# Shared-key attention (L1_ffn) as one stage, from gate logits to the layer norm

## The reference, cut to what matters

```python
x = _layernorm(x + _L1_ffn_ref(x, L1_ffn_W_gate, L1_ffn_W_qkv))   # H = 16 heads, hd = 16

gating = softmax(x @ W_gate.T)
idx = argmax(gating);  indicator = one_hot(idx, H)
gating_top1 = indicator * max(gating)
q, k, v = split(x @ W_qkv.T, 3)
k_shared = einsum('bth,bthd->btd', indicator, k)      # each token picks one head's key
v_shared = einsum('bth,bthd->btd', gating_top1, v)    # and value, weighted
att = softmax(causal(einsum('bhqd,bkd->bhqk', q, k_shared) / sqrt(hd)))
y = einsum('bhqk,bkd->bhqd', att, v_shared)
```

## Time and profile before

| | us |
|---|---|
| median of 3 runs | 2063.25 (2061.75 to 2067.89) |
| the profiled execution | 2062.26 |
| its span, first to last instruction | 2060.4 |
| PE / DVE / ACT / POOL busy | 1655.1 / 1342.0 / 1060.9 / 576.6 |
| mean granted clock of TensorE | 0.867 |
| L1_ffn with its layer norm | 1155.05 to 1319.56 |

### The profile page before, as it was taken

How to read it: one execution, slowest core, us unless ns; L and a number is a source line. 1 busy time by engine, 2 the same in 40 slices (tenths; PEclk the granted TensorE clock), 3 DMA queues, 4 the chain that set the end, 5 groups by cost and what they waited for, 6 DMA issues and landing times. The chain is left out here.

```text
span 2060.4 us, 28503 instructions
## 1 busy us (share of the span) xinstructions
PE 1655.1 (80%) x9533; PEld 1038.3 (50%) x9541; DVE 1342.0 (65%) x2664; ACT 1060.9 (51%) x2192; POOL 576.6 (28%) x466
## 2 busy tenths in 40 slices
PE   7957899999997879998489759875999777458924
PEld 3743566666775536655366447552222334216712
DVE  4767777676764448884577365346999647824467
ACT  2024556555543248894268348425999622515525
POOL 0406342322100018891121000003990000406710
PEclk9989999999999989999789869997555669778959
DMA  4000000000001001110000000007999600020000
GB/s 201 27 1 26 1 1 1 1 1 1 1 1 43 16 22 52 43 50 1 16 2 2 26 1 2 24 1 215 172 181 189 116 21 5 0 82 1 2 0 21
DMA packets 163008, 80.67 MB, mean 39 GB/s; under 512 B 155280, under 2 KB 156432, under 8 KB 161200
## 3 DMA queue, kind: packets, MB, share of 16 engines
q1 hardware_dynamic: 162720, 78.46, 15.9%
q10 hardware_dynamic: 144, 0.39, 0.0%
HBM read 39.44 MB, written 1.11 MB: 20 GB/s over the span
## 5 line engine op out<-in xcount | busy, mean ns | idle before, releaser
L1213 POOL TENSOR_TENSOR ss_u<-dx,b_rows 128x512 f32<-128x512 f32 x128 | 159.1, 1277 | 241.7 <-POOLq L181 225.7
L2034 ACT ACTIVATE qc_p<-qc_s,qc_bias,sq 128x1024 int16<-128x1024 f32 x128 | 154.2, 1204 | 16.5 <-DVE qc_bias L2000 6.4
L1295 DVE TENSOR_TENSOR_SCAN ss_h<-ss_decay,ss_u 128x512 f32<-128x512 f32 x128 | 146.5, 1204 | 24.2 <-PE ss_ht L1253 18.4
L932 ACT ACTIVATE gq_p<-gq_s,gq_bias,gq_rq 128x512 f32<-128x512 f32 x128 | 98.4, 773 | 119.2 <-DVE gq_bias L1002 119.2
L1998 DVE TENSOR_REDUCE qc_mx<-qc_s 128x1 f32<-128x1024 f32 x128 | 155.4, 1214 | 4.8 <-PE qc_s L1933 4.7
L865 POOL TENSOR_TENSOR gq_xw<-gq_x,weights 128x512 f32<-128x512 f32 x48 | 67.8, 1413 | 295.2 <-ACT gq_x L892 294.5
L1933 PE MATMUL qc_s<-kT,qT 64*128 64x512 bf16 x256 | 130.8, 617 | 15.0 <-ACT qc_p L2034 7.3
L1267 PE MATMUL ss_acc<-ss_hc,consts 128*128 128x512 f32 x256 | 130.8, 594 | 0.0
L800 PE MATMUL gq_s<-gq_KT,gq_QT 128*128 128x512 f32 x256 | 121.9, 599 | 3.6 <-ACT gq_p L932 3.6
L822 PE MATMUL gq_o<-gq_pT,gq_V 128*128 128x256 f32 x512 | 121.2, 379 | 1.4 <-DVE gq_pT L1036 1.4
L999 DVE TENSOR_REDUCE gq_mx<-gq_s 128x1 f32<-128x512 f32 x128 | 88.2, 691 | 43.9 <-PE gq_s L800 43.5
(11 more groups left out here) (579 smaller groups left out, 4121.9 us busy)
## 6 DMA issues: line engine op xcount, KB each, us to landing
b_rows<-b_rows SPq DMA_DIRECT2D x16, 512.0 KB, 3.7
weights<-in_weights SPq DMA_DIRECT2D x1, 6152.0 KB, 17.9
weights<-in_weights SPq DMA_DIRECT2D x1, 5248.0 KB, 16.7
...
qc_pT<-qc_p SPq DMA_TRANSPOSE x128, 3.3
...
```

The lines of the kernel that those rows point to most:

```text
L932: nc.scalar.activation(pr[c % 2][:, t, :], sc[t][:, :], ACT.Exp, bias=bias[:, c, t:t + 1], scale=rq[b % 2][:, t, u:u + 1], accum_out=sm[:, ...
L1213: nc.gpsimd.tensor_tensor(u_in[i % 3][:, :], dx[:, m, hf * HT:hf * HT + HT], rows.rows[c % 2][:, n % rows.NEACH, :], ALU.mult).then_inc(in ...
L1295: nc.vector.tensor_tensor_scan(h[group % 2][:, m, :], decay[i % 2][:].rearrange("p b t -> p (b t)"), u_in[i % 3][:, :], 0.0, ALU.mult, ALU ...
L2034: nc.scalar.activation(pi[i % R][:, :], sc[i % 3][:, :], ACT.Exp, bias=bias[:, i:i + 1], scale=sq[:, t, h:h + 1], accum_out=sm[:, i:i + 1] ...
```

## The change

The seven stages of L1_ffn become one, with the layer norm in it.

- PE starts with the gate logits of all eight tiles, into a part of the bank that later holds turned outputs (`plg`). Then three key and value products (`select`), then in turn a query product (`query`), a key and value product and a key transpose (`turn_key`), the rest of the transposes, and the core's loop as before.
- DVE chooses heads from the logits in PSUM (`choose_heads`), now with the softmax weight folded into `eqv`, then for each tile multiplies the key and value product, still in PSUM, by `eq` and `eqv` and reduces (`pick`). No key and value copy is made.
- ACT stores all queries, repeats keys (`repeat`) and stores turned keys (`store_key`), in its list one behind the other. GpSimd makes the masked keys, 32 pieces of 256 elements; the scores wait for theirs.
- The value weight has a 17th column of ones, so that the output products give the sum of the exponentials too. The exponentials lose their accumulator; the reciprocal is taken of the turned outputs.
- `Finish` does the norm: the first half's part stands between the last two steps of DVE's loop, the rest behind it. The stage names 34 semaphores, and `FUSED` gets entry 5.

Most removed lines are left out here; they are in the functions above.

```diff
--- before.py
+++ after.py
@@ -1527,116 +1527,80 @@
-def L1_ffn(g, W):
+def L1_ffn(g, W, weights):
     nc = g.nc
+    U = B * 16
+    wqkv, wg = W("wqkv", 2), W("wg", 2)
     with ExitStack() as ctx:
         sb, pb = places(g, ctx)
-        vs = sb("vs", [P, NT, 16])
...
-            dense(g, jobs, "f1")
-            pick_heads(g, lg, kv, ks, vs)
-            dense(g, transpose_jobs(g, rep, kT, ct=1), "f1t")
-        shared_core(g, qT, km, vs)
-def pick_heads(g, lg, kv, ks, vs):
...
+        sc = [pb(f"sh_s{i}", [P, 512]) for i in range(3)]
+        ptb = [pb(f"sh_t{i}", [P, 512]) for i in range(2)]
+        pt = [t[:, 0:384].rearrange("p (a b) -> p a b", a=3) for t in ptb]
+        plg = pot[:].rearrange("p t h d -> p (t h d)")[:, 0:128].rearrange("p (t h) -> p t h", t=NT)
+        qT, km, kT = sb("sh_q", [P, 2, TOK]), sb("sh_km", [P, 8, TOK]), sb("sh_k", [P, TOK])
+        vs, ks = sb("sh_vs", [P, NT, 17]), sb("sh_ks", [P, NT, 16])
+        mxl, sml, top = (sb(f"sh_l{n}", [P, NT]) for n in ("mx", "sum", "top"))
+        e, eq, eqv = (sb(f"sh_l{n}", [P, NT, 16]) for n in ("e", "eq", "eqv"))
+        big = [sb(f"sh_big{i}", [P, 2, 16, 16]) for i in range(2)]
+        rep = [sb(f"sh_rep{i}", [P, P]) for i in range(2)]
+        mx = sb("sh_mx", [P, U, 2])
+        rs = [sb(f"sh_rs{i}", [P, 2, 4]) for i in range(2)]
+        with stage(g, "sh_logits sh_kv sh_q sh_qstored sh_shifted sh_lexp sh_lchain sh_big sh_picked sh_rep sh_kturned sh_kstored "
+                      "sh_masked sh_ones sh_zeroed sh_scored sh_max sh_exp sh_turned sh_copied sh_used sh_out_stored "
+                      "sh_out_turned sh_recip sh_normed " + Finish.NAMES) as (
...
+            fin = Finish(g, ctx, sems, [], [sc[0], sc[1]])
+            def select(t):
+                if t >= 3:
+                    nc.tensor.wait_ge(chosen, 2 * t - 4)
+                for k in range(2):
+                    last = nc.tensor.matmul(sc[t % 3][:, :], g.XT[:, k, t * P:t * P + P], wqkv[:, k, 256:768], start=(k == 0),
+                                            stop=(k == 1))
+                last.then_inc(kv, 1)
+            def query(j):
+                m, n = j // 2, j % 2
+                if j >= 2:
+                    nc.tensor.wait_ge(qstored, j - 1)
+                for k in range(2):
+                    last = nc.tensor.matmul(ptb[j % 2][:, :], wqkv[:, k, m * P:m * P + P], g.XT[:, k, n * 512:n * 512 + 512],
+                                            start=(k == 0), stop=(k == 1))
+                last.then_inc(queries, 1)
+            def turn_key(t):
+                nc.tensor.wait_ge(repeated, t + 1)
+                if t >= 2:
+                    nc.tensor.wait_ge(kstored, t - 1)
+                nc.tensor.transpose(po[t % 2][:, 0:P], rep[t % 2][:, :], g.ident).then_inc(kturned, 1)
             def scores(u):
                 b, h = u // 16, u % 16
-                if u >= 3:
+                if u < 3:
+                    nc.tensor.wait_ge(chosen, 2 * NT)
+                else:
                     nc.tensor.wait_ge(exped, 2 * (u - 2))
+                if h < 8:
+                    nc.tensor.wait_ge(masked, 8 * b + h + 1)
                 for t in range(2):
                     s = sc[u % 3][:, QS[t]]
                     nc.tensor.matmul(s, qT[:, h // 8, b * S + t * P:b * S + t * P + P],
...
-                    nc.tensor.matmul(po[i % 2][32 * h:32 * h + 16, :], vs[:, 2 * b, :],
+                    nc.tensor.matmul(po[i % 2][32 * h:32 * h + 17, :], vs[:, 2 * b, :],
                                      prT[(4 * i + h) % 8][:, 0:2, :].rearrange("p a b -> p (a b)"), start=True, stop=False)
                 for h in range(4):
-                    last = nc.tensor.matmul(po[i % 2][32 * h:32 * h + 16, P:S], vs[:, 2 * b + 1, :],
+                    last = nc.tensor.matmul(po[i % 2][32 * h:32 * h + 17, P:S], vs[:, 2 * b + 1, :],
...
@@ -1678,6 +1643,21 @@
             @block.tensor
             def _(pe):
+                for t in range(NT):
+                    for k in range(2):
+                        last = nc.tensor.matmul(plg[:, t, :], g.XT[:, k, t * P:t * P + P], wg[:, k, :], start=(k == 0),
+                                                stop=(k == 1))
+                last.then_inc(logits, 1)
+                for t in range(3):
+                    select(t)
+                for j in range(4):
+                    query(j)
+                    select(3 + j)
+                    turn_key(j)
+                select(7)
+                for t in range(4, NT):
+                    turn_key(t)
+                pe.wait_ge(qstored, 4)
+                fin.turn(0)
+                fin.turn(1)
             @block.scalar
             def _(act):
+                def store_query(j):
+                    m, n = j // 2, j % 2
+                    act.wait_ge(queries, j + 1)
+                    nc.scalar.activation(qT[:, m, n * 512:n * 512 + 512], ptb[j % 2][:, :], ACT.Copy,
+                                         scale=0.25).then_inc(qstored, 1)
+                def repeat(t):
+                    act.wait_ge(picked, t + 1)
+                    if t >= 2:
+                        act.wait_ge(kturned, t - 1)
+                    nc.scalar.copy(rep[t % 2][:, :].rearrange("p (r d) -> p r d", r=8), mid(ks[:, t, :], 8)).then_inc(repeated, 1)
+                def store_key(t):
+                    act.wait_ge(kturned, t + 1)
+                    nc.scalar.copy(kT[:, t * P:t * P + P], po[t % 2][:, 0:P]).then_inc(kstored, 1)
+                act.wait_ge(shifted, 1)
+                nc.scalar.activation(e[:], e[:], ACT.Exp).then_inc(lexp, 1)
+                for t in range(NT + 1):
+                    if t < 4:
+                        store_query(t)
+                    if t < NT:
+                        repeat(t)
+                    if t >= 1:
+                        store_key(t - 1)
...
                             nc.scalar.activation(pr[i % 4][:, QS[t]], sc[i % 3][:, QS[t]], ACT.Exp,
-                                                 bias=mx[:, i, t:t + 1],
-                                                 accum_out=sm[:, i, t:t + 1]).then_inc(exped, 1)
-                nc.vector.tensor_copy(ob[i % 2][:, :], po[i % 2][:, :]).then_inc(out_stored, 1)
-                nc.vector.wait_ge(exped, 8 * i + 8)
-                nc.vector.reciprocal(sm[:, 4 * i:4 * i + 4, :], sm[:, 4 * i:4 * i + 4, :]).then_inc(recip, 1)
...
+                                                 bias=mx[:, i, t:t + 1]).then_inc(exped, 1)
+                fin.root(0)
+                fin.store(0)
+                fin.root(1)
+                fin.store(1)
+            @block.gpsimd
+            def _(pool):
+                nc.gpsimd.memset(vs[:, :, 16:17], 1.0).then_inc(ones_made, 1)
+                for b in range(B):
+                    pool.wait_ge(kstored, 2 * b + 2)
+                    for j in range(8):
+                        nc.gpsimd.tensor_scalar(km[:, j, b * S:b * S + S], kT[:, b * S:b * S + S], g.eighth[:, j:j + 1], None,
+                                                ALU.mult).then_inc(masked, 1)
             @block.vector
             def _(dve):
+                link = Count(dve, lchain)
+                def choose_heads():
+                    dve.wait_ge(logits, 1)
+                    link(nc.vector.tensor_reduce(mxl[:, :], plg, AX.X, ALU.max))
+                    nc.vector.tensor_tensor(e[:], plg, bcast(mxl[:, :], 16), ALU.subtract).then_inc(shifted, 1)
+                    link(nc.vector.tensor_tensor(eq[:], plg, bcast(mxl[:, :], 16), ALU.is_equal))
+                    link(nc.vector.tensor_tensor(eq[:], eq[:], mid(g.rank, NT), ALU.mult))
+                    link(nc.vector.tensor_reduce(top[:, :], eq[:], AX.X, ALU.max))
+                    link(nc.vector.tensor_tensor(eq[:], eq[:], bcast(top[:, :], 16), ALU.is_equal))
+                    dve.wait_ge(lexp, 1)
+                    link(nc.vector.tensor_reduce(sml[:, :], e[:], AX.X, ALU.add))
+                    link(nc.vector.reciprocal(sml[:, :], sml[:, :]))
+                    link(nc.vector.tensor_tensor(eqv[:], eq[:], bcast(sml[:, :], 16), ALU.mult))
+                def pick(t):
+                    dve.wait_ge(kv, t + 1)
+                    if t >= 2:
+                        dve.wait_ge(picked, t - 1)
+                    for j, weight in enumerate((eq, eqv)):
+                        nc.vector.tensor_tensor(big[t % 2][:, j], sc[t % 3][:, j * 256:j * 256 + 256].rearrange("p (h d) -> p d h", h=16),
+                                                mid(weight[:, t, :], 16), ALU.mult).then_inc(chosen, 1)
+                    dve.wait_ge(chosen, 2 * t + 2)
+                    nc.vector.tensor_reduce(vs[:, t, 0:16], big[t % 2][:, 1], AX.X, ALU.add)
+                    nc.vector.tensor_reduce(ks[:, t, :], big[t % 2][:, 0], AX.X, ALU.add).then_inc(picked, 1)
+                def store_out(i):
+                    dve.wait_ge(used, i + 1)
+                    if i >= 2:
```

(31 more changed lines are left out.)

100 lines of the change are left out of this document (9 added, 91 removed).

## The result

The changed kernel takes 2041.6 us (median of 4 runs, 2041.25 to 2044.2), the kernel before 2065.57 in the same rounds (4 runs, 2061.75 to 2070.67); the ratio is 0.9885, 95% interval 0.9860 to 0.9911. Measured again beside the last experiment it is 2043.15 against 2066.87 (0.9886, 0.9871 to 0.9900). Both pairs of medians differ by some 24 us. I had said 20.3.

What follows compares the result with a forecast made beforehand. The sublayer's head was taken as bound by its order, the core by TensorE. Head -21.8, filling -0.6, core 0, tail +0.4 and next sublayer +1.7 sum to -20.3 from 2062.3: 2042 us, range 2038 to 2046.

Steps and rivals of the forecast that it cites:

- Logits: Start of the sublayer's head: 32 records of 16 columns, now first, take 6.9 us at clock 0.50, like the router's dense.
- Products and chain: Rest of the head: PE done at 1185.3, scores 32.8 us after the start instead of 54.6, 21.8 us gained.
- Picks: DVE head choice per tile: 1.9 us with its wait, hidden under PE's 3.6 us a tile except behind the last products.
- rival of dear PSUM reads: In the head, picks from PSUM cost 1.0 instead of 0.5 us a product, giving 2044; chance 0.12.
- Masks: 32 masks of 256 elements on POOL: 0.35 to 0.7 us each, first eight ended by 1182, cost 0.
- Filling: First scores to steady period of the core: clock falls soon after scores begin, 0.6 us gained, ends 0 and 3.1.
- Core: Removed accumulator reads, 17-column output products and PE's mask waits together change the core by 0 us.
- in a slack of 4 us: In the core, the reciprocal on DVE after the turn instead of beside it: 0.2 us, covered by this slack.
- Tail: Last outputs' copy to next sublayer: 10.0 us of work plus 3.3 of exit, 13.3 against 12.9, 0.4 us lost.
- 0.075 us a semaphore: At a stage's exit, each semaphore above ten costs about this; the exit with 34 takes 3.3 us.
- The next sublayer: Its products start at half clock behind a 3.3 us exit: 1.7 us lost, ends 0 and 3.4.
- kinder clock: Clock rises within the logits, stays up into the core and is up for the next sublayer: 2034.5; chance 0.20.

Runs made afterwards that it cites:

- the last experiment: Changed kernel with mixed logit order, six idle products and 19 semaphores instead of 34, timed beside the unaltered changed kernel: 2040.61 us against 2043.15.
- e4_reorder: Changed kernel with three key and value products ahead of the gate logits and two query products behind them: head 31.81 us against 31.69.
- e10_strides_before: Kernel before, with the values' eight picks reading SBUF in storage order instead of with the stride: head 53.35 us, 1.23 less.
- e6_waits4: Changed kernel with TensorE waiting for masks four times instead of 32: scores to last copy 94.49 us against 94.48.
- e7_late: Changed kernel with eight unused DVE products ahead of the last pick: 2055.25 us, head 34.59.
- e5_accum: Changed kernel with the exponentials writing their accumulated sums again, into a tile nothing reads: 2040.88 us.
- e2_sems20: Changed kernel with 20 more semaphores named in its stage that nothing uses: 2044.2 us.
- e11_fewer_warm: Changed kernel with logits mixed between wide products, six idle TensorE products at the end and 19 semaphores instead of 34: 2040.61 us, ratio 0.9872 to before.
- e9_warm: Changed kernel with mixed logit order and nine idle TensorE products in the gaps at the sublayer's end: next sublayer 68.28 us against 68.50 without them.
- e3_unfused: Changed kernel with the layer norm as a stage of its own again and 27 semaphores in the attention stage: 2041.63 us.

## Why the prediction was right, point by point

**Logits, right**: 6.82 us at 0.50 for 6.9. The row of the router was the right neighbour, and e4_reorder shows that the work's shape brings the clock down even from 1.00.

**Products and chain, right and a little dear**: PE's last product ended 29.4 us after the start for 30.25, the chain behind it took 2.29 for 2.55. Together 22.9 us gained where I said 21.8.

**Picks, right in what they cost the head**: a pick of 1.64 us for 1.9, DVE idle for 9.0 us in front of them. The rival of dear PSUM reads did not come true (425 and 414 ns for its 1.0 us), and e10_strides_before shows that it was the strided SBUF reads that were dear.

**Masks, mis-sized and harmless**: 922 ns each, above my upper end of 0.7; they start at 1184.1 and end by 1213, hidden, and e6_waits4 shows that even the first eight are in time. But the margin was luck: I had the first eight start 21 us into the head and end 6 us ahead of the scores; they start 23.6 us into it and end 0.9 us ahead. I had taken 697 ns for 512 elements as an upper end for 256, and 256 took longer. Why was not tried.

**Filling, the step that failed**: "I take a fall soon after the scores begin, 0.6 us gained". It gained 3.2, my upper end of 3.1. The fall that I took over from the earlier trace rows came some 1 us after the old dense had ended, so it was not the long stand behind that brought it. Ahead of it ran 3.6 us of logits, the narrow products that bring the clock down in e4_reorder; that they did so here too is inferred, not tried. Here wide products stood ahead, and PE then stood for some 1.4 us of the chain's 2.3, at most 0.96 at a time. e7_late lets it stand for 3.74 and gets the fall and the 6.34 us. I had the number, "2.5 us with four transposes", and took neither from it how little of it is standing nor from the row what had run before. The size is less firm than the step: cold fillings took 5.5 to 6.6 us, the warm one 3.45.

**Core, nearly**: 87.83 for 87.22, 0.6 lost where I said 0. ScalarE's relief is worth nothing (e5_accum), the mask waits cost nothing (e6_waits4), the products with 17 columns cost the same. The 0.6 stands in the list of waits as three output transposes that wait for DVE's copy, 0.2 us each, and three of the periods of four units, one behind each of the first three batch elements, take 6.0 us in place of 5.8: "in a slack of 4 us" was wrong where the reciprocal, the sum and the statistics of a batch element come together ahead of the copy. That the reciprocal is the cause was not tried by itself.

**Tail, right in sum**: 12.91 for 13.3, as before. DVE's and ACT's part took 9.9 us for 10.0, the exit 2.97 for 3.3. The 0.075 us a semaphore was right up from 34 (0.07 in e2_sems20) and dear down from 34 (0.04 to 0.06 in e11_fewer_warm).

**The next sublayer, right and a little low**: 2.2 us lost where I said 1.7. It ran at half clock from its first product: 0.52 over 1299.64 to 1303.60, then 1.00, where before it was at 1.00. With the clock held through the tail, the standing at the exit decided: 2.96 us were enough for the fall in e9_warm, 1.90 were not in e11_fewer_warm. Yet in e3_unfused and in the kernel before 1.51 us stood in front of the next sublayer, behind the same sixteen transposes at 0.50, and one started cold and the other at 1.00. So the exit alone is not the rule, and what else goes into it stays open.

The sum of the parts is -22.9 - 3.2 + 0.6 + 0 + 2.2 = -23.3 for -20.3, nearly all of the difference from the filling and the head. The medians moved by 24.0 and 23.7. My 2042.0 met the median of 2041.6 closer than its parts deserve, and that is luck, since it stood on the profiled 2062.26 and the kernel before ran at 2065.57 in the rounds that counted. The kinder clock, a rival at 0.20, came true in one of its three parts: not in the logits, in the filling, not in the next sublayer.
